# Logits of a Swin block from one stacked product per head and image

## The reference

```python
y = roll(ln(x) * g1 + b1, (-3, -3))            # windows of 7 x 7 = 49 tokens, 64 per image
q, k, v = split(y_windows @ qkv_w.T + qkv_b)   # 16 heads of 8 channels
attn = (q * 8 ** -0.5) @ k.T                   # 49 x 49 per window and head
attn = softmax(attn + bias[head] + mask[window])
o = roll((attn @ v) @ proj_w.T + proj_b, (3, 3))
x = x + o
out = x + gelu(ln2(x) @ fc1_w.T + fc1_b) @ fc2_w.T + fc2_b
```

## Time and profile before

| | |
|---|---|
| median of three runs | 4031.51 us (4028.34 to 4037.39) |
| profiled execution, first to last instruction | 4042.2 us |
| TensorE, matmul busy | 3761.8 us, 93% |
| TensorE, weight loads busy | 2946.3 us, 73% |
| VectorE busy | 3171.0 us, 78% |
| ScalarE busy | 2782.5 us, 69% |
| GpSimd busy | 2985.0 us, 74% |
| mean granted TensorE clock | 0.992 |
| transfers | 442.02 MB, mean 109 GB/s |

### The profile page before, as it was taken

The page is one execution under the profiler, slowest core; times in us unless marked ns, Lnnn a source line. Parts: engine busy times, 40 slices in busy tenths (PEclk is TensorE's granted clock), DMA queues, the critical chain, the costliest instruction groups (busy, mean ns, idle before and its releaser), DMA issues. The chain is left out here.

```text
span 4042.2 us, 177003 instructions
## 1 busy us (share of the span) xinstructions
PE 3761.8 (93%) x75664; PEld 2946.3 (73%) x75664; DVE 3171.0 (78%) x7840; ACT 2782.5 (69%) x3840; POOL 2985.0 (74%) x3988
## 2 busy tenths in 40 slices
PE   2899999999999999999999999999999999999997
PEld 1677777777777777777777777777777777777776
DVE  6787887787778777878887787788888778788774
ACT  1677677677677767766776676677677677777674
POOL 5677777777777777777777777777777777777775
PEclk8999999999999999999999999999999999999998
DMA  2333333333333333333333333333333333333331
GB/s 78 102 112 116 110 111 115 112 111 113 113 109 108 115 110 111 107 113 111 111 117 111 106 111 113 111 112 117 111 112 116 111 111 114 114 110 112 113 107 56
DMA packets 609604, 442.02 MB, mean 109 GB/s; under 512 B 142083, under 2 KB 608371, under 8 KB 608819
## 3 DMA queue, kind: packets, MB, share of 16 engines
q1 hardware_dynamic: 608355, 428.88, 35.8%
q0 software_dynamic: 464, 1.81, 0.1%
HBM read 106.14 MB, written 51.46 MB: 39 GB/s over the span
## 5 line engine op out<-in xcount | busy, mean ns | idle before, releaser
L610 DVE TENSOR_REDUCE neg_max<-ps 113x16 f32<-113x784 f32 x1024 | 999.8, 976 | 591.9 <-PE ps L773 477.0
L433 ACT ACTIVATE probs<-ps 113x784 f32<-113x784 f32 x1024 | 848.2, 828 | 789.2 <-PE ps L808 577.5
L402 POOL TENSOR_TENSOR hid_lo<-probs,hid_hi 128x784 f16<-128x784 f32 x512 | 919.7, 1817 | 75.3 <-DVE hid_hi L604 75.3
L808 PE MATMUL ps<-st_q,st_k 128*49 128x196 f16 x8192 | 696.3, 249 | 0.0
L803 PE MATMUL ps<-bias,eye_k 106*64 106x392 f16 x4096 | 686.2, 331 | 0.0
L773 PE MATMUL ps<-mx_k,mx_q 128*49 128x196 f16 x8192 | 544.0, 253 | 68.8 <-DMA mx_q<-q_hi 32.9
L604 DVE CAST hid_hi<-probs 128x784 f16<-128x784 f32 x512 | 492.6, 982 | 112.1 <-ACT probs L448 111.6
L808 PEld LDWEIGHTS ps<-st_q,st_k 128*49 128x49 f16 x8192 | 446.5, 105 | 122.3 <-issue 0.5
L448 ACT ACTIVATE probs<-ps,col 128x784 f32<-128x784 f32 x512 | 468.0, 914 | 88.9 <-PE ps L837 59.8
L855 PE MATMUL ps<-w_hi,hid_hi 128*112 128x128 f16 x3584 | 524.3, 227 | 4.3 <-DVE hid_hi L604 3.5
L855 PE MATMUL ps<-w_lo,hid_hi 128*112 128x128 f16 x3584 | 501.6, 220 | 0.0
(11 more groups left out here) (118 smaller groups left out, 7703.2 us busy)
## 6 DMA issues: line engine op xcount, KB each, us to landing
st_k<-k_hi SPq DMA_DIRECT2D x256, 196.0 KB
st_q<-q_hi SPq DMA_DIRECT2D x1024, 49.0 KB
oT_raw<-pv_sb SPq DMA_DIRECT2D x256, 196.0 KB, 3.5
x_in<-in_x SPq DMA_DIRECT2D x224, 196.0 KB
x_res<-in_x SPq DMA_DIRECT2D x224, 196.0 KB
out_y<-y_out SPq DMA_DIRECT2D x224, 196.0 KB
mx_k<-k_hi SPq DMA_DIRECT2D x512, 49.0 KB
mx_q<-q_hi SPq DMA_DIRECT2D x128, 196.0 KB
```

The costliest lines, as they stand in the source:

```text
L402: nc.gpsimd.tensor_tensor(hid_lo[:, c, :], hid[:, c, :], hid_hi[:, c, :], ALU.subtract).then_inc(s_hid_lo, 1)
L433: nc.scalar.activation(probs[0:KP, w % 4, :].rearrange("p (b c) -> p b c", b=2), ps[0:KP, b:b + 2, 0:HB * WT], ACT.Exp).then_inc(s_exp, 1)
L610: nc.vector.tensor_reduce(neg_max[0:KP, :, :, w].rearrange("p e g -> p g e"), ps[0:KP, 0:2, :].rearrange("p b (g c) -> p (b g) c", g=2)[:, ...
L808: last = mm(group(im, bank, g, EQ * WT), st_k[par][:, g, span], st_q[par][:, :, g, span], start=False, stop=(g % 2 == 1))
```

## The change

Each head gets its own rows in `st_k` and `st_q`, now both [128, 16 heads, 784]. From 0 to 105 in steps of 15 (`HIGH_ROWS`) stand the eight channels of hi·hi; between them, 14 rows at a time, the key identity in `st_k` against the bias in `st_q` (two parts: 49 rows high, 49 rows low); rows 106 to 109 the mask; rows 110 to 125 (`CROSS_ROWS`) the terms hi·lo and lo·hi; row 126 the row maxima against ones. One 49 x 49 product over the first 127 rows gives the logits of one head and image, complete. The rough product is the same with the first 110 rows, and roles of the two operands exchanged as before, so `mx_k`, `mx_q`, `eye_k` and the bias product are gone. Per w there are 32 products of 49 columns for the logits and 32 for the maxima.

The bias rows, identities and masks are put in place once in the set-up (two broadcast loads of `k_fixed` issued by ACT, two copies by DVE, mask loads by SP); the masks are loaded again for the first two bottom bands. Per turn SP now issues 2 transfers of the high rows, 4 of the cross rows and 1 of the row maxima. Exp takes a scale per row, 1 for rows of tokens and 0 for the unused ones, and more of PSUM is cleared at the start.

```diff
-GQ, EQ = 4, 4
 HP = 64
-MAX_ROW = 3
-MASK_ROWS = 2 * WT
-BIAS_ROWS = MASK_ROWS + 8
+ROW_STEP = 2 * WS + 1
+HIGH_ROWS = slice(0, ROW_STEP * (HD - 1) + 1, ROW_STEP)
+MASK_ROWS = slice(ROW_STEP * (HD - 1) + 1, ROW_STEP * (HD - 1) + 5)
+MAX_K = MASK_ROWS.stop
+CROSS_ROWS = tuple(slice(MAX_K + term, MAX_K + 2 * HD - 1 + term, 2) for term in range(2))
+MAX_ROW = MAX_K + 2 * HD
+CORE_K = MAX_ROW + 1
...
-        st_q = [sb(f"st_q{e}", [C, EQ, GQ, 2 * BT], F16) for e in range(2)]
-        st_k = [sb(f"st_k{e}", [C, GQ, 2 * BT], F16) for e in range(2)]
-        neg_max = sb("neg_max", [C, EQ, NG, NW])
+        st_q, st_k = ([sb(f"{n}{e}", [C, NH, 2 * BT], F16) for e in range(2)] for n in ("st_q", "st_k"))
+        neg_max = sb("neg_max", [C, NH, NW])
...
+        N_MX, N_ST, N_NEG, N_O, N_SUM, N_RR = (16 * k for k in (2, 4, 1, 2, 2, 2))
...
-            for strips, table in ((strips_k, table_k), (strips_q, table_q)):
-                lines = table.rearrange("h (a b) -> (h a) b", b=2 * WS - 1)
-                for j in range(WS):
-                    sp.dma_start(strips[j].rearrange("h (a b) -> (h a) b", b=WS),
-                                 lines[:, WS - 1 - j:2 * WS - 1 - j]).then_inc(s_bd1, 16)
+            lines = table_k.rearrange("h (a b) -> (h a) b", b=2 * WS - 1)
+            for j in range(WS):
+                sp.dma_start(strips_k[j].rearrange("h (a b) -> (h a) b", b=WS),
+                             lines[:, WS - 1 - j:2 * WS - 1 - j]).then_inc(s_bd1, 16)
...
-            sp.wait_ge(s_bd1, 16 * 2 * WS)
+            sp.wait_ge(s_bd1, 16 * WS)
             sp.wait_ge(s_zero, 1)
             for i in range(WS):
                 span = slice((WS - 1 - i) * WS, (WS - 1 - i) * WS + WT)
-                for copy in range(2):
-                    r = copy * WT + WS * i
+                for part in range(2):
+                    r = ROW_STEP * i + 1 + part * WS
                     sp.dma_start(bias_k[r:r + WS, :, :], strips_k[:, :, span]).then_inc(s_bd2, 16)
-                r = 32 * (i // 3) + 1 + i % 3
-                sp.dma_start(bias_q[r:r + 4 * WS:4, :, :], strips_q[:, :, span]).then_inc(s_bd2, 16)
-            sp.dma_start(bias_k[MASK_ROWS:BIAS_ROWS, :, :], classes_q).then_inc(s_bd2, 16)
-            r = 32 * (WS // 3) + 1 + WS % 3
-            sp.dma_start(bias_q[r:r + 4 * 8:4, :, :], classes_k).then_inc(s_bd2, 16)
-
-            def neg(n, heads, par):
-                for e in heads:
-                    row = 32 * e + MAX_ROW
-                    sp.dma_start(st_q[par][row:row + 1, e, :, :].rearrange("p g c -> p (g c)"),
-                                 neg_maxT[32 * e:32 * (e + 1), :, :]).then_inc(s_neg_dma, 16)
+            sp.wait_ge(s_init, 2)
+            for e in range(2):
...
-                    neg(n, (0, 1), odd(0))
+                    sp.dma_start(st_q[odd(0)][MAX_ROW:MAX_ROW + 1, :, :].rearrange("p h c -> p (h c)"),
+                                 neg_maxT[:, :, :]).then_inc(s_neg_dma, 16)
...
-                n = t
-                if exists(n):
-                    neg(n, (2, 3), odd(0))
                 n = t + 1
                 if exists(n):
 
-                    if past(n, 0):
-                        sp.wait_ge(s_rows, NW * n)
-                    else:
-                        sp.wait_ge(s_init, 2)
-                        sp.wait_ge(s_initp, 1)
-                    sp.wait_ge(s_hi, 2 * n + 1)
-                    for e in range(EQ):
-                        sp.dma_start(mx_k[32 * e:32 * (e + 1):4, :, e, :],
-                                     k_hi[32 * e:32 * (e + 1), :, :, :].rearrange("c w m q -> c (w m q)")
-                                     ).then_inc(s_mx_dma, 16)
-                    sp.wait_ge(s_hi, 2 * n + 2)
-                    sp.dma_start(mx_q[edge(n)][0:C:4, :, :],
-                                 q_hi[:, :, :, :].rearrange("c w m q -> c (w m q)")).then_inc(s_mx_dma, 16)
+                    if past(n, 1):
+                        sp.wait_ge(s_st, NW * (n - 1))
+                    elif n == 0:
+                        sp.wait_ge(s_k_fixed, 16 * 2)
+                    if n - EDGE in (0, 1):
+                        for st, masks in ((st_k, k_masks[0]), (st_q, q_masks[1])):
+                            sp.dma_start(st[odd(1)][MASK_ROWS, :, :].rearrange("p h c -> p (h c)"),
+                                         masks).then_inc(s_mask, 16)
+                    for j, (st, high) in enumerate(((st_k, k_hi), (st_q, q_hi))):
+                        sp.wait_ge(s_hi, 2 * n + j + 1)
+                        sp.dma_start(st[odd(1)][HIGH_ROWS, :, :],
+                                     high[:, :, :, :].rearrange("c w m q -> c (w m q)")).then_inc(s_mx_dma, 16)
                 n = t - 3
                 if exists(n):
                     sp.wait_ge(s_fin, 2 * (n + 1))
@@ -310,18 +295,14 @@
                 n = t + 1
                 if exists(n):
 
-                    if past(n, 1):
-                        sp.wait_ge(s_st, NW * (n - 1))
                     if past(n, 0):
                         sp.wait_ge(s_st_dma, N_ST * n)
-                    sp.wait_ge(s_lo, 2 * (n + 1))
-                    for term, (qq, kk) in enumerate(((q_hi, k_hi), (q_hi, k_lo), (q_lo, k_hi))):
-                        sp.dma_start(st_k[odd(1)][term:C:4, :, :],
-                                     kk[:, :, :, :].rearrange("c w m q -> c (w m q)")).then_inc(s_st_dma, 16)
-                        for e in range(EQ):
-                            sp.dma_start(st_q[odd(1)][32 * e + term:32 * (e + 1):4, e, :, :],
-                                         qq[32 * e:32 * (e + 1), :, :, :].rearrange("c w m q -> c (w m q)")
-                                         ).then_inc(s_st_dma, 16)
+                    for j, terms in enumerate((((st_k, 1, k_hi), (st_k, 0, k_lo), (st_q, 0, q_hi)),
+                                               ((st_q, 1, q_lo),))):
+                        sp.wait_ge(s_lo, 2 * n + j + 1)
+                        for st, term, part in terms:
+                            sp.dma_start(st[odd(1)][CROSS_ROWS[term], :, :],
+                                         part[:, :, :, :].rearrange("c w m q -> c (w m q)")).then_inc(s_st_dma, 16)
...
             for dst, src in ((idn, ident), (own, own_rows), (is_part, parts), (sel, spread)):
                 pool.dma_start(dst[:, :], src).then_inc(s_const, 16)
-            pool.dma_start(eye_k[:, :, :, :], eye).then_inc(s_const, 16)
-            for e in range(2):
-                pool.dma_start(mx_q[e][:, :, :], mxq_fixed[e]).then_inc(s_const, 16)
             nc.gpsimd.memset(half[:, :], -0.5)
             for e in range(2):
-                nc.gpsimd.memset(st_q[e][:, :, :, :], 0.0)
                 nc.gpsimd.memset(yT_hi[e][:, :, :, :], 0.0)
-                nc.gpsimd.memset(yT_lo[e][:, :, :, :], 0.0)
-                last = nc.gpsimd.memset(st_k[e][:, :, :], 1.0)
+                last = nc.gpsimd.memset(yT_lo[e][:, :, :, :], 0.0)
...
         def _(act):
+            for e in range(2):
+                act.dma_start(st_k[e][:, :, :], k_fixed.unsqueeze(1).to_broadcast([C, NH, 2 * BT])).then_inc(s_k_fixed, 16)
...
                 nc.scalar.activation(probs[0:KP, w % 4, :].rearrange("p (b c) -> p b c", b=2),
-                                     ps[0:KP, b:b + 2, 0:HB * WT], ACT.Exp).then_inc(s_exp, 1)
+                                     ps[0:KP, b:b + 2, 0:HB * WT], ACT.Exp,
+                                     scale=own[0:KP, 2:3]).then_inc(s_exp, 1)
...
-            nc.vector.memset(hid[:, 0:2, :], 0.0).then_inc(s_zero, 1)
+            nc.vector.memset(hid[:, 0, :], 0.0).then_inc(s_zero, 1)
...
             nc.vector.memset(bv_wide, 0.0)
-            nc.vector.memset(ps[:, 0:2, :], 0.0)
+            nc.vector.memset(ps[:, 0:6, :], 0.0)
...
             then(nc.vector.tensor_scalar(part_lo, part_lo, is_part[:, 1:2], None, ALU.mult))
             then(nc.vector.scalar_tensor_tensor(part_hi, part_hi, is_part[:, 0:1], part_lo, ALU.mult, ALU.add))
-            nc.vector.tensor_copy(bias[:, :, :].rearrange("p b c -> p (b c)"), part_hi)
-            then(nc.vector.tensor_copy(mx_k[:, :, :, :].rearrange("p g e (u k) -> p (g e) u k", k=WT),
-                                       bias_q.unsqueeze(2).to_broadcast([C, NH, 2 * NW, WT])))
-            nc.vector.tensor_copy(part_lo[:, 0:1], own[:, 0:1]).then_inc(s_init, 2)
+            for e in range(2):
+                nc.vector.tensor_copy(st_q[e][:, :, :].rearrange("p h (u q) -> p h u q", q=WT),
+                                      part_hi.rearrange("p (h q) -> p h q", h=NH).unsqueeze(2).to_broadcast(
+                                          [C, NH, 2 * NW, WT])).then_inc(s_init, 1)
 
...
                     dve.wait_ge(s_maxT, n)
                 nc.vector.tensor_reduce(
-                    neg_max[0:KP, :, :, w].rearrange("p e g -> p g e"),
-                    ps[0:KP, 0:2, :].rearrange("p b (g c) -> p (b g) c", g=2)[:, :, 0:EQ * WT].rearrange(
```

(80 more changed lines are left out.)

34 lines of the change are left out of this document (9 added, 25 removed).

## The result

The changed kernel takes 5086.91 us (median of 4 runs, 5072.2 to 5099.84), the kernel before, beside it, 4034.45 us (4 runs, 4028.34 to 4040.69): a ratio of 1.2605, with an interval of 1.2583 to 1.2628. Forecast were 3794 us, within 3715 to 3900. It came out slower by 26%, beyond both rivals on the slow side (4464 and 4617). The profiled execution has a span of 5070.4 us at a mean granted clock of 0.931.

What follows compares the result with a forecast made beforehand. TensorE, 93% busy and gapless in the loop, was taken as the bound. Loop 212 us, q's transfer 15 and set-up 10 made 237 off 4042: 3805 profiled, 3794 us as median, range 3715 to 3900.

Steps and rivals of the forecast that it cites:

- p: Time from one pair of 49-column products (one per image) to the next; taken as 24 ns, bounds 20.4 and 45.
- E: Slower rival, 4%: one product start per 25 ns over the whole array, p = 50, 4617 us.
- the forecast's sum: Length of the loop over eight windows: 7.85 + 240p, 13.61 us at p = 24 ns, before 15.27.
- the first step: First maxima product at w = 0, waiting for DVE's x1: stays 1.08 us after the logits.
- rival A: Main case, 70%: gains as forecast, p between 22 and 26 ns, 3709 to 3880 us.
- D: Slower rival, 9%: next 49-column weights can't load under the current product, p = 45, 4464 us.
- The part ahead: Transposes, fc1 and projections before each turn's loop: 14.98 us, forecast at 15.0 as before.
- The wait for x1: TensorE waiting for DVE's x1 at w = 0: near 0.4 us instead of 0.20.
- The wait for q's transfer: TensorE's 32.9 us of waiting in total: between 0 and 33 gained, 15 taken, no such wait left.
- Exp: ScalarE's exp with a scale per partition: 0 to 0.09 us longer than 0.82, lying beside TensorE.
- DVE's ring: Maxima product, DVE reduction, next maxima product: 1.62 us against TensorE's round of 1.72, keeping up by 0.10.
- The gain of 10 us: Set-up with fewer memsets, strips and bias transfers but added loads: 0 to 15 us earlier, 10 taken.

Runs made afterwards that it cites:

- the micro kernel: TensorE alone, computing nothing of the reference: stages of 49-, 98- and 196-column, fp32 and 128 x 128 products; 49-column stage 54.4 us, fp32 stage 58.2 us.
- the kernel without the three transfers: Changed kernel without three of its four cross-row transfers per turn (k high, k low, q high); 4881.67 us, ratio 1.2083.
- the cut kernel (49 columns): Kernel before, with each logits and maxima product of 196 columns issued as four of 49; 5039.1 us, ratio 1.2482.
- 98-column pieces: Kernel before, with each logits and maxima product of 196 columns issued as two of 98; 4249.75 us, ratio 1.0532.

## Why the prediction was wrong

**The step that failed** is "That is a weight load and a matmul every 11 ns, so issue allows p = 22". The 11 ns were read from one burst of 64 records, that is half a block, and they hold within a block: in the micro kernel's fp32 stage 128 records last 1.59 us at their fastest, (1.59 - 0.2) / 127 = 11 ns each, but blocks begin 3.45 to 4.0 us after each other. Neither that burst nor any other row of before says how fast blocks follow each other; the 9.6 us of "issue" at L823 were the only trace of it. The profile had a sum that could have raised the question: 402 products in 15.27 us were 4.9 us per block, and the change asked for 2.3. From p on, the working counts only what TensorE does with instructions that it has. No rival had this mechanism: E priced a start every 25 ns over the array, p = 50. Measured by supply, a block at 3.5 to 3.8 us is 27 to 30 ns per product, a p of 55 to 60, but over all instructions of the loop, P·V and fc2 too, and not over the 49-column products alone.

**Sizes.** A group of 32 products lasts 0.60 to 0.61 us (forecast 0.55), so (0.61 - 0.192) / 31 = 13.5 ns each and p = 27, not 24; the micro kernel gives the same. Put into the forecast's sum, that makes 7.85 + 240 x 0.027 = 14.3 us instead of 13.6. The change from group to group is a little cheaper than the sum has it, though. Read from start to start where no stall falls, maxima to logits takes 0.44 us (2569.73 to 2570.17; forecast 0.41), logits to P·V or fc2 0.52 (0.48), the last maxima to P·V 0.54 (0.51); P·V 0.83, fc2 0.81 and the first step 1.08 are as forecast. That adds up to 14.1 us, 1.2 less than before, 154 us in all in place of 212. So without the stalls the loop would have come out within rival A's p of 22 to 26. D's serial load (p = 45) and E's start every 25 ns over the array (p = 50) are refuted: 13.4 ns from start to start leave no room for either.

**The part ahead** was right: 14.98 us in the turn shown, 14.01 against 13.91 in the mean. **The wait for x1** was right: 0.47 us at w = 0 (0.4 forecast), 59.9 us in all. **The wait for q's transfer** fell from 32.9 to 14.2 us, so the 15 was about that size, but four waits remain where none was forecast; the longest, 5.5 us, is in the set-up. **Exp** took 911 ns, 83 more than before (828), near the upper bound of the 0 to 0.09, and costs nothing here, since it waits for TensorE (921 us of its idle time are for L739). **DVE's ring** hardly bound: TensorE waited 10.8 us for the reductions, 10.6 before. How it would do at the intended pace was not seen.

**Set-up.** The gain of 10 us did not come. TensorE's transposes (L852) begin at 50.50 where L884 began at 54.12, but the first maxima product begins later than before, 71.22 against 66.55, behind the transfer of q:

```profile
71.22 0.94 PE L739 MATMUL ps<-st_k,st_q 110*49 110x49 f16 x32 [5.53 <-DMA st_q<-q_hi]
```

Half of these 4.7 us is that q goes out later (66.69 against 64.26), since the first projection waits 9.8 us for DVE's yT_lo; the other half is that 4.5 us pass from its issue to the product, where it was 2.3.

**Where the 1052 us are.** Without supply stalls the loop would have been some 1.2 us shorter than before; it is 7.84 us longer. The difference is 9.0 us, or 1157 in all. Of it, 881 us is idle "issue" behind the set-up. The rest is work at half clock beside it: the mean granted clock fell from 0.992 to 0.931, which is 2 x 0.069 x 5070 = 700 us at the 1.2 GHz level, and by the trace's clock records TensorE was busy for 555 of them, where half the time would have done at the higher level, an estimated loss of 277. (The kernel before has 13 and 20 us of the two.) The lower clock goes with the long stalls: in the kernel without the three transfers, with no stall over 2.5 us, the mean is 0.954, in the cut kernel (49 columns) 0.976. The same account divides the transfers' 205 us: without them "issue" behind the set-up is 750 us, 130 less, and TensorE is busy at the lower level for 410 us, a loss of 205, 73 less. What stays open is why the few-partition form holds a packet of instructions back; that it does is shown, the way is not.

## What to carry to other kernels

Count TensorE's instructions per time, not only its columns. A weight load and a matmul are two, and a block of 256 came at best every 3.45 us with nothing beside it and every 3.5 to 3.9 us in this kernel. So here a stretch of several blocks was bound by supply where the mean product was shorter than about 28 ns (3.6 us / 128), and cutting or "un-stacking" products cost time even with no column added. The page gives the check before any edit: products of the stretch / 128, times 3.6 us, against its length. It has to be made for each dense stretch: with 98-column pieces the loop as a whole needed only 530 / 128 x 3.6 = 14.9 us of supply, less than its 15.3, but two windows asked for a block every 3.4 us, and the kernel lost 5%. Where the count binds, an edit that halves the instructions pays for them too: P·V in fp16, one pass for two, gave 8.0% in the changed kernel, and 5.4% in the kernel before, where only its columns counted.

## What the runs showed of the hardware

- Alone on the core, a block of 128 weight loads and matmuls came at best every 3.45 us (16 blocks in 54.4 us, the first of them in part ready), and every 3.7 to 4.3 us beside other traffic at 208 GB/s.
- After the packet of a block has landed, TensorE goes on with it about 1.4 us later (micro and changed kernel alike).
- Supply runs only a little ahead. After the part ahead of the loop, 14.98 us with 197 products, the loop ran 150 products until its first stall (2563.93 to 2568.50). So a long light stretch bought little more than one block for the dense one behind it.
- Transfers of 196 KB into eight partitions run at 103 GB/s, into 128 partitions at 208, and beside the first kind TensorE stalls for 4 to 7 us before some blocks.
- 49-column fp16 products on alternating halves of the array follow each other at 13.4 ns, 27 ns per half, with a new weight load each time. The Trainium skill ("TensorE: Matmul & The Clock Gate", section "Wait — 56ns, not 53.3ns?") has about 25 ns as a floor; it agrees with these rows for each half, not for the array.
